# Three row maxima, the ranks and six weight-block transposes moved around the last expert of a mixture-of-experts layer

## What is computed

```python
edge_index = jnp.stack([src, dst])
x = x + _L0_gnn_ref(_layernorm(x, axis=-1), edge_weight, L0_gnn_bias, edge_index)
x = x + _L0_ffn_ref(_layernorm(x, axis=-1)[None], L0_ffn_wg, L0_ffn_w1, ...)[0]
x = x + _L1_gnn_ref(_layernorm(x, axis=-1), edge_index, L1_gnn_W, L1_gnn_b)
x = x + _L1_ffn_ref(_layernorm(x, axis=-1)[None], L1_ffn_w1, L1_ffn_w2)[0]
```

## Time and profile before

| what | us |
|---|---|
| median of three runs | 1056.78 |
| lowest and highest of them | 1055.4, 1057.2 |
| profiled execution, first to last instruction (its span) | 1054.4 |
| TensorE busy in it | 979.3 (93%) |
| VectorE busy | 737.9 (70%) |
| ScalarE busy | 467.1 (44%) |
| GpSimd busy | 128.0 (12%) |
| mean granted TensorE clock, of full speed | 0.977 |

### The profile page before, as it was taken

How to read it: one execution, slowest core, us unless ns; L and a number is a source line. 1 busy time by engine, 2 the same in 40 slices (tenths; PEclk the granted TensorE clock), 3 DMA queues, 4 the chain that set the end, 5 groups by cost and what they waited for, 6 DMA issues and landing times.

```text
span 1054.4 us, 17446 instructions
## 1 busy us (share of the span) xinstructions
PE 979.3 (93%) x6781; PEld 533.9 (51%) x6781; DVE 737.9 (70%) x1038; ACT 467.1 (44%) x573; POOL 128.0 (12%) x139
## 2 busy tenths in 40 slices
PE   1799899996899999999969999899999999999998
PEld 0688655553555666665534444444444444444444
DVE  7999888877664555668679754999977555555541
ACT  5344446553355565566522113999733122222221
POOL 6300042320311111000043100011000000000000
PEclk9899899998899999999989999999999999999999
DMA  3800026665778898885446855788513554444441
GB/s 121 243 2 2 2 81 227 244 228 193 233 293 306 324 350 323 318 320 204 159 162 182 215 128 178 278 319 310 186 40 71 120 120 113 109 109 109 110 98 36
DMA packets 166145, 188.91 MB, mean 179 GB/s; under 512 B 126520, under 2 KB 126842, under 8 KB 161984
## 3 DMA queue, kind: packets, MB, share of 16 engines
q1 hardware_dynamic: 159679, 165.47, 49.1%
q0 software_dynamic: 6400, 22.55, 6.5%
HBM read 137.98 MB, written 35.33 MB: 164 GB/s over the span
## 4 chain that ended last, share of the span: by engine, by line
PE 74%; DVE 14%; issue 6%; DMA 3%; ACT 2%; POOL 0%; DVEq 0%; SPq 0%; ACTq 0%; POOLq 0%
PE ps L1095 20%; PE ps L1293 13%; PE ps L1322 12%; PE ps L1202 8%; PE ps L1218 6%; DVE fq L2276 3%; PE ps L1275 2%; PE ps L1159 2%; DMA eo_d<-eo 2%; DVE w1l L2111 2%; PE ps L982 1%; PE ps L955 1%; DVE stats L1775 1%; PE ps L973 1%; DVE o_key L1854 1%
## 5 line engine op out<-in xcount | busy, mean ns | idle before, releaser
L1293 PE MATMUL ps<-w1q,xqt 128*128 128x512 fp8e4 x640 | 139.9, 379 | 0.4 <-issue 0.4
L1656 ACT ACTIVATE hf<-ps,fs 128x512 f32<-128x512 f32 x80 | 54.9, 688 | 183.2 <-PE ps L1293 183.2
L1322 PE MATMUL ps<-w2q,hqt 128*128 128x512 fp8e4 x576 | 126.4, 379 | 0.0
L2360 DVE TENSOR_REDUCE hm<-hf 128x1 f32<-128x512 f32 x80 | 54.2, 685 | 73.8 <-ACT hf L1656 73.8
L1293 PEld LDWEIGHTS ps<-w1q,xqt 128*128 128x128 f16 x640 | 62.4, 98 | 75.8 <-issue 0.9
L1322 PEld LDWEIGHTS ps<-w2q,hqt 128*128 128x128 f16 x576 | 56.3, 98 | 66.9
L1095 PE MATMUL ps<-wt_h,xt 128*128 128x512 f16 x320 | 85.4, 379 | 0.0
L1095 PE MATMUL ps<-gwt_h,xt 128*128 128x512 f16 x320 | 84.5, 379 | 0.6 <-issue 0.6
L1202 PE MATMUL ps<-xdh,w1h 128*128 128x314 f16 x256 | 77.1, 301 | 6.2 <-ACT ht L1566 3.3
L1202 PE MATMUL ps<-xdh,w1l 128*128 128x314 f16 x256 | 76.4, 299 | 0.0
L1202 PE MATMUL ps<-xdl,w1h 128*128 128x314 f16 x256 | 76.3, 298 | 0.0
(11 more groups left out here) (320 smaller groups left out, 1949.5 us busy)
## 6 DMA issues: line engine op xcount, KB each, us to landing
wstage<-in_L_ffn_w SPq DMA_DIRECT2D x32, 1024.0 KB, 10.9
abs_in<-in_L_ffn_w SPq DMA_DIRECT2D x18, 1024.0 KB, 6.5
abs_e<-in_L_ffn_w SPq DMA_DIRECT2D x14, 1024.0 KB, 5.1
fnat_b<-in_L_ffn_w SPq DMA_DIRECT2D x28, 512.0 KB, 6.4
fnat_a<-in_L_ffn_w SPq DMA_DIRECT2D x27, 512.0 KB, 4.8
eo_d<-eo SPq DMA_DIRECT2D x16, 512.0 KB, 3.1
hq_d<-hq SPq DMA_DIRECT2D x8, 1024.0 KB, 6.3
xs_d<-xs_all SPq DMA_DIRECT2D x10, 512.0 KB, 2.9
```

The costliest lines, as they stand in the source:

```text
L1293: last = mm(ps[:, n % 4, :], xqt[:, u, k, :], w1q[:, k // 2, n * 512:(n + 1) * 512, k % 2], start=(k == 0), stop=(k == KD - 1))
L1322: last = mm(ps[:, 4 + h, :], hqt[:, u, k, :], w2q[:, k // 2, h * 512:(h + 1) * 512, k % 2], start=(k == 0), stop=(k == KF - 1))
L1656: cp(hf[:, i % 2, n * 512:(n + 1) * 512], ps[:, n % 4, :], ACT.Gelu, scale=fs[:, i % 2, 3:4]).then_inc(s_ge, 1)
L2360: last = v.tensor_reduce(hm[:, u, n:n + 1], hf[:, u, n * 512:(n + 1) * 512], AX.X, ALU.max, apply_absolute_value=True)
```

## The change

On VectorE the maxima of tiles 7, 8 and 9 move from the end of expert 6 to a place ahead of expert 0. `ranks` moves from behind the second output eviction of the last expert to behind its sixth and last. On TensorE only blocks 0 and 1 are turned between the output groups, and blocks 2 to 7 behind the last group; the three `ranked` stay behind blocks 4, 5 and 6. VectorE's copies of blocks 2 and 3 and the low parts of blocks 4 and 5 move behind the ranks. On SyncE the loads of blocks 4 and 5 stay behind the first store of `eo`, and the loads of 6 and 7 move from behind the second store to behind the four stores of the last 58 rows.

```diff
@@ SyncE, expert(e, ep)
-                        if last_of(e, NE):
-                            w1_rows(4 + 2 * s)
-                            w1_rows(5 + 2 * s)
+                        if last_of(e, NE) and s == 0:
+                            w1_rows(4)
+                            w1_rows(5)
...
                         sp.dma_start(rest[:, 512:D], eo[64 + 48:64 + SM[s], u, 512:D]).then_inc(s_eoh[u], 16)
+                        if last_of(e, NE):
+                            w1_rows(6)
+                            w1_rows(7)
@@ TensorE, expert(e, ep)
                         if last_of(e, NE):
-                            w1_t(2 * s + h)
+                            if s == 0:
+                                w1_t(h)
...
                 if last_of(e, NE):
-                    for i in range(4, KD):
+                    for i in range(2, KD):
                         w1_t(i)
-                        if i < KD - 1:
+                        if 4 <= i < KD - 1:
                             ranked(i - 4, (6, 7, 3)[i - 4])
@@ VectorE, last_expert(e, ep)
                 for n in range(4):
                     result_rows(e, ep, n // 2, n % 2)
-                    w1_part(n)
-                    w1_low(2 + n)
-                    if n == 1:
-                        ranks()
+                    if n < 2:
+                        w1_part(n)
+                        w1_low(2 + n)
                 result_rows(e, ep, 2, 0)
                 result_rows(e, ep, 2, 1)
-                for i in range(4, KD):
+                ranks()
+                for i in range(2, KD):
                     w1_part(i)
                     if i + 2 < KD:
                         w1_low(i + 2)
@@ VectorE, expert(e, ep)
                 if isinstance(e, int):
-                    for b in range(NE - 1, NT):
-                        low_rows(b)
                     dve.wait_ge(s_cmax, NT)
@@ VectorE, ahead of pairs(dve, expert, NE)
             dve.wait_ge(s_dinv2, 2)
+            for b in range(NE - 1, NT):
+                low_rows(b)
```

## The result

The changed kernel takes **1060.28 us** (median of five runs, 1059.35 to 1062.37) against 1055.5 (five runs, 1054.56 to 1057.2): ratio 1.005, 95% interval 1.0038 to 1.0063, or 5.3 us (4.0 to 6.6); the two medians lie 4.8 us apart. The forecast was slower by 2.6 us, counted from 1056.78, the median of the first three runs of the kernel before: 1059.4, range 1056.4 to 1061.8. Direction and range held; the size did not.

A forecast was written before the change was run, and what follows sets the result against it. The prediction took the start of the third layer's product as the bound, set by the second `mixed`. The six-block tail (+1.7) and block 7's load (+0.9) sum to +2.6 us on 1056.78: 1059.4, range 1056.4 to 1061.8.

The forecast's parts named there:

- What bounds: Start of the third layer's product: set by gathers landing last before; after the change, by VectorE's weight copies.
- Maxima: Three maxima leave the last expert's VectorE work: 0.55 us gained on TensorE, cost 0 in expert 0.
- Two blocks fewer: Between the last expert's output groups: last group 2.9 us earlier; last evictions, stores and gathers 3.45 us earlier.
- The head of the tail: Behind the last group: block 3's low squares wait behind ranks and block 2's copy; block 4 turned 3.5 us later.
- The whole schedule without transfers and clock: Tail of six blocks up to the second `mixed`: +1.7 us, the least if no transfer is late.
- The failed step: Tail from block 4's squares to VectorE's last weight copy: unchanged work, 10.4 us.
- TensorE's shorter stop may keep its clock up: TensorE's stop before the product: possibly a help to its clock, no size given, since VectorE's path leads up to 543.
- The term of the load: Block 7's load on SyncE's queue beside the gathers: landing after 5.3 us instead of 4.4, +0.9 us.
- The sum: Second `mixed`, product's start and span: 1.7 + 0.9 = +2.6 us, giving 1059.4.
- rival 4: Block 7's load much later, landing after 6.5 to 8 us: 1060.6 to 1062.0, chance 0.11.
- case 3: Main case, block 7's load slowed in the gathers' company: 1058.9 to 1060.6, chance 0.38.

The follow-up runs named there:

- e11_added: The kernel before with three extra maxima ahead of expert 0, whose results nobody waits for: ratio 1.0009.
- e1_maxima: The kernel before with only the three maxima moved ahead of expert 0: ratio 1.0011.
- e5_filler_early: The changed kernel with filler matmuls in TensorE's three tail stops and the loads of blocks 6 and 7 issued early into their own buffer: ratio 1.0026.
- e2_filler: The changed kernel with filler matmuls, results unread, in TensorE's three stops in the tail: ratio 1.0051.
- e3_ranks_back: The changed kernel with the ranks back behind the second output eviction, maxima and blocks still moved: ratio 1.0021.
- e6_max_ranks: The kernel before with the maxima moved and the ranks behind the last two evictions, four blocks in the tail as before: ratio 1.0036.
- e10_gathers_held: e2_filler with GpSimd's gathers held until block 7's load has landed: stretch from last expert's first output matmul to product's start 46.78 us, one run.

## Why the prediction was right, and where not

**What bounds.** Right. The gathers no longer end last; the weight side does, and the product's 112 us are what they were.

**Maxima.** Right. First `htl` at 495.08 (forecast 494.5), no cost to be seen in expert 0 (e11_added), a gain of 0.4 to 0.7 in the stretch (e1_maxima, forecast 0.55).

**Two blocks fewer.** Right. Counted from the first output matmul, which is 0.35 later in this execution, the last group starts at 12.48 (512.75 - 500.27) where the forecast had 512.4 - 499.92 = 12.48, and its evictions at 15.37 against 15.28. GpSimd issued its first gather at 520.60, forecast 521.5; it came earlier because the stores of `eo` in front of it landed sooner than the forecast had taken over from the kernel before (the 96 KB ones after 1.9 us instead of 3.5). It was indeed worth nothing.

**The head of the tail.** Right. The low squares of block 3 waited 1.68 (forecast 1.9), and block 4 was turned at 21.68, forecast 21.68. The whole schedule without transfers and clock, +1.7, was measured at +1.6 (e5_filler_early).

**The failed step** is the sentence "From there the work is what it was, blocks 4 to 7 with three `ranked` between: 518.06 to 528.43, 10.4 us". It took 12.96. I took durations measured on a TensorE that had not stopped and set them behind the stops that the change makes. My own sum had two of the three, 1.9 us before block 3's low squares and 1.25 before block 4 (520.35 to 521.6); measured are 1.26, 1.68 and 1.26. At half clock block 4 and the first `ranked` cost 2.6 us more. The clock stood in the prediction only once, and with the wrong sign: "TensorE's shorter stop may keep its clock up". That looked at the stop behind 528 and not at the new ones. Its reason for leaving the clock out, that the path up to 543 is VectorE's, missed that VectorE's last copy waits for TensorE's last squares.

**The term of the load** was mis-sized as well. Taken at 5.3 us, it was 6.3 in the kernel after and 7.0 and 7.2 in e2_filler and e3_ranks_back. The case was named, the row for the price was the wrong one: the gathers' landing beside each other. With the gathers held the same load took 5.0. The Trainium skill (DMA: Bandwidth & Descriptors, "Queues, rings and completion order") lets a DMA engine take turns between its queue rows; worked out ahead of the result this gave a landing after 6.0 us. The trace agrees in kind, 6.3 to 7.2 beside the gathers and 5.0 with them held, though no view shows the turns themselves. By that rule the sum would have been +3.3, nearer to the 4.25 measured, but for a reason that did not act alone: in the kernel after the clock's 2.6 covered the load's delay.

**The sum.** On the stretch: +1.6 for the schedule and +2.6 for two delays that overlap, of which either alone would do; forecast 1.7 + 0.9. On the stretch, +4.25, the change fell where rival 4 had it (3.8 to 5.2 above 1056.78), with the mechanism of rival 4 (the load at 6.5 to 8) present but not alone. The median, 1060.28, lies in the span of case 3, but only because five runs of the kernel before gave 1055.5 and not 1056.78. Case 3 was too small, and no case had the clock. That the time lies inside the range is in part luck: the range was not drawn for this cause, and 5.3 us on 1056.78 would be 1062.1, just outside it.

**What stays open.** The totals of the kernels with the maxima moved stand 1.0 to 1.9 us above what their stretches explain (after: 5.3 against 4.25; e1_maxima 1.2 against -0.7), except e3_ranks_back, which stands 1.8 below. The place ahead of expert 0 shows no cost in e11_added's rows, and that kernel's ratio, 1.0009 (0.9991 to 1.0027), neither shows nor excludes one of such a size. The stretches come from one execution each, so parts of a few tenths of a microsecond are not shown. Why the clock falls behind one pattern of stops and not behind another is open too.

## What to carry to other kernels

When an edit puts short waits into a stretch where TensorE worked through, price the work behind them also at half clock: what the waits themselves cost is only the first part. When a load is moved to where other queues are at work, price it with the slowest transfer seen in such company and not with the middle one (6.7 for the gathers in the earlier trace rows, against the 5.3 that was taken and the 6.3 to 7.2 that came). And when a mend gives nothing, don't drop its cause: look for a second one of the same length beside it, and try the two together.

## What was unexpected of the hardware

The clock fell without any long stop. In the kernel after, stops of 1.26 and 1.68 us, with squares of 0.61 us behind each, were followed by its fall to half inside 520 to 521, about when the third stop began (520.7). In e6_max_ranks it fell at the end of one stop of 3.27. With stops of 0.96, 1.26 and 1.26 (e3_ranks_back) it did not fall there, but later, within three microseconds of the start of the stop of 2.08 (528.87). In the kernel before it fell latest: TensorE, busy nearly throughout up to then, ended its last squares at 528.4, and the clock was 1.00 up to 533, as the stretches of before show:

```profile
532.00:533.00 1.00, 0.00 (x0) 0.00 (x0) 0.70 (x1) 0.00 (x0) 0.00 (x0) 1.00 0.95 336
533.00:534.00 1.00, 0.00 (x0) 0.00 (x0) 0.85 (x2) 0.00 (x0) 0.00 (x0) 0.73 0.85 348
534.00:536.00 2.00, 0.27 (x1) 0.14 (x2) 1.81 (x5) 0.00 (x0) 0.33 (x1) 0.50 0.13 53
```

So the half clock came about five microseconds into one unbroken stop there (528.4 to 533.5), and about four behind the start of the first short stop here (516.5 to 520.6).

A 512 KB load on SyncE's queue landed after 3.6 us where it went ahead of the gathers' data (block 6, after), after 5.0 with the gathers held (block 7, e10_gathers_held) and after 6.3 to 7.2 beside them (block 7, three kernels), one execution each.
